# A two-layer convolution and attention kernel on one core: low halves in other groups, the projection bias in the norm, and a patch scratch ordered by row tile

## The chip, the core and the metric

The kernel runs on one core of a Trainium2 chip. TensorE (PE in the profile; PEld is its weight load), VectorE (DVE), ScalarE (ACT), GpSimd (POOL) and SyncE (SP) each work through their own list of instructions in order and meet at semaphores. DMAs are issued from SP and, for a few stores, from ACT; both kinds run on the same 16 DMA engines. The metric is the device time of one execution in microseconds, the median of several.

## The reference

Two layers on an image x of 384 channels by 192 by 192, in float32. Cut to what matters:

```python
# layer 0: x = x + L0(_gn(x)), _gn is a group norm over 32 groups of 12 channels
qkv = einsum('bchw,oc->bohw', x, w_qkv) + b_qkv          # 384 -> 1152 channels
qkv = qkv.reshape(b, 3*c, 96, 2, 96, 2).max(axis=(3, 5)) # 2 x 2 maximum
qkv = depthwise 3 x 3 convolution (w_dw) + b_dw
q, k, v = split(qkv, 3); q, k = q / norm(q), k / norm(k)
attn = einsum('bhcn,bhdn->bhcd', q, k) * temperature     # 8 heads of 48 channels
out = sum of 4 top-k softmaxes of attn, each @ v * a_i
out = gelu(out); out = repeat 2 x 2 of out; out = einsum('bchw,oc->bohw', out, w_proj) + b_proj
# layer 1: x = x + L1(_gn(x))
out = bn(dwconv 13 x 13) + bn(dwconv 3 x 3) + bn(x)      # depthwise, bn with given statistics
```

## The kernel before

The stages run one after another, with a barrier between them: the statistics of x, the affine part of the group norm (`group_affine`, "g0"), the q/k/v stage (`stage_qkv`), the attention matrix, the projection stage (`stage_project`), the second group norm ("g1"), the kernels and constants of the depthwise stage (`stage_kernels`), and the depthwise stage. All orders are written out by hand, as loops that every engine walks with its own waits.

**The q/k/v stage.** The image is cut into 24 tiles of 8 rows (1536 pixels). A step t handles two tiles, 2t and 2t+1, and there are 12 steps. A step has 36 slots, four for each of the 9 groups of 128 output channels. In slot s TensorE makes 18 matmuls (L724) of 384 columns into one of two banks `qbank[s % 2]`: two row pairs, three input blocks, and three products (high x high, high x low, low x high) since weights and pixels are split into two float16 halves, "high" and "low". It may start slot s when VectorE's maximum of slot s-2 is through. VectorE then does in slot s: the 2 x 2 maximum of the bank (`largest`, L631), one tap each of the two channel groups in work (`tap`, L644), and in six slots of the 36, given by `LOW_AT`, the low half of one input block (`low`, L623: xlo = xf - xhi). TensorE has more to do in some slots: the gram matmuls (`GRAM_AT`: behind slots 3 and 5) and the transposes of q and k behind slots 15, 19, 23, 27, 31 and 35.

One input block goes round a single buffer `xf[:, b]`: SP loads it (`load`, L298), ScalarE normalises it in place (`norm`, L472, slots by `NORM_AT`), writes its high half (`high`, L481, `HIGH_AT`), VectorE writes the low half, and this `lo_ready` lets SP load the same block of the next tile. ScalarE also does bias and tap 0 of every group (`first_tap`, L501 and L514), which VectorE's tap 1 waits for, the halo rows, the evacuation of the transposes (`turned`), and pieces of the 13 x 13 kernels (`bands`). In an entry `8: (0, 1)` of these tables 8 is the slot, 0 the half (tile 2t+2 or 2t+3) and 1 the block. Before the first step SP also fills most of the Toeplitz scratch in DRAM with zeros, six DMAs of 2048 runs each from `blank` (L426); in the before kernel they stand ahead of the loads of tile 2.

**The projection stage.** 24 steps of one tile of 8 rows. The list `ORDER` gives the sequence on TensorE and ScalarE. "A" n is attention times v into `abank[n]` and ScalarE's gelu of it (L1092, L1007); "Y" n is the projection into `ybank[n]` (L1101), three matmuls over the input blocks, and ScalarE's bias on it in place (L1010); "T" n is one of 12 runs of up to four 128 x 128 transposes (L1078) of the tile before (4, 4, 4 and 1 per channel block) into one of two banks `tbank[n % 2]`, and ScalarE's copy of it to `turned` (L995). T n on TensorE waits for the copy of T n-2. VectorE adds x and the projection for block b (four adds, L1027), when Y b has its bias and the four T of block b are through, then takes statistics (L1032). SP stores `turned` for each block to the patch scratch (L962), the copy of T 0, 4 or 8 waits until the store before of that block has landed, and SP loads v and x two tiles ahead (L891, L892) once the adds of the step are through.

**The depthwise stage.** 24 groups of 16 channels. A group is loaded from the patch scratch into `raw` in one DMA (`load_group`, L1199), two groups ahead; SP then issues one Toeplitz load per channel (L1293), eight channels ahead. TensorE makes 18 matmuls per channel (L1453) and nine fills of four transposes per group (L1434).

## Time and profile before

| | us |
|---|---|
| median of 3 runs | 3161.54 |
| lowest and highest run | 3158.27 and 3162.66 |
| the profiled execution, its own time | 3158.36 |
| its span, first to last instruction | 3156.6 |
| busy: PE, DVE, ACT | 2745.8, 2437.0, 1408.2 |
| mean DMA rate over the span | 179 GB/s |

A busy time is the union of an engine's instructions. Consecutive matmuls overlap in the records (one takes 0.33 us, and the next starts 0.16 us later), so PE's busy time counts the stream and not its single pieces. The stages are best read as stretches of the span: the q/k/v stage ends near 1640 us, the projection stage reaches from 1692 to 2130, and the depthwise stage begins at 2174.

### The profile page before, as it was taken

How to read it: one execution, taken by the hardware profiler on the slowest of the kernel's cores; microseconds unless marked ns; L12 is line 12 of the kernel's file. 1: busy time of each engine (PE TensorE's matmuls, PEld its weight loads, DVE VectorE, ACT ScalarE, POOL GpSimd, SP SyncE). 2: the span in 40 equal slices, each digit the busy share in tenths (PEclk: the TensorE clock that was granted, in tenths of full speed). 3: DMA queues.
4: the chain of work that ended last, by engine and by line, in shares of the span. 5: the costliest groups of instructions: out<-in, count | busy, mean ns of one | idle time of the engine just before them, and what ended most of it. 6: DMA issues, size and time to landing. Idle time of an engine off the chain costs nothing. (4 is left out here: it accounts for less than half of the span.)

```text
span 3156.6 us, 51308 instructions
## 1 busy us (share of the span) xinstructions
PE 2745.8 (87%) x18393; PEld 2009.8 (64%) x18393; DVE 2437.0 (77%) x3335; ACT 1408.2 (45%) x1799; POOL 27.5 (1%) x43
## 2 busy tenths in 40 slices
PE   0049999999999999999965888875999999999998
PEld 0035665665665665665643555544999999999998
DVE  7938899989989989999976888866666666666663
ACT  0024445455545555543223777773444444444442
POOL 0010000000000000000000000000000000000000
PEclk9999999999999999999987999986999999999999
DMA  9961112112112112111005999977999998889986
GB/s 359 415 239 60 47 41 81 55 50 82 54 50 82 54 50 82 54 49 36 16 19 193 324 319 318 327 253 212 279 283 277 281 284 283 280 276 282 283 254 185
DMA packets 231368, 565.73 MB, mean 179 GB/s; under 512 B 30928, under 2 KB 137008, under 8 KB 228144
## 3 DMA queue, kind: packets, MB, share of 16 engines
q1 hardware_dynamic: 213936, 496.89, 49.2%
q10 hardware_dynamic: 17280, 66.85, 5.6%
q8 instruction: 91, 1.49, 0.2%
q14 instruction: 61, 0.50, 0.1%
HBM read 402.95 MB, written 160.73 MB: 179 GB/s over the span
## 5 line engine op out<-in xcount | busy, mean ns | idle before, releaser
L1453 PE MATMUL cv_cb<-cv_hi,cv_toep 128*128 128x288 f16 (+1 forms) x4608 | 910.1, 290 | 31.6 <-DVE cv_lo L1387 29.0
L724 PE MATMUL qk_qb<-qk_xhi,whi 128*128 128x384 f16 x2592 | 847.9, 327 | 75.3 <-DVE qk_pool L631 61.0
L644 DVE SCALAR_TENSOR_TENSOR qk_dw<-qk_pool,qk_wd,qk_dw 128x768 f32<-128x768 f32 (+2 forms) x864 | 836.4, 1008 | 25.1 <-ACT qk_dw L514 25.0
L724 PE MATMUL qk_qb<-qk_xlo,whi 128*128 128x384 f16 x2592 | 847.3, 327 | 0.0
L724 PE MATMUL qk_qb<-qk_xhi,wlo 128*128 128x384 f16 x2592 | 847.0, 327 | 0.0
L1453 PE MATMUL cv_cb<-cv_lo,cv_toep 128*128 128x288 f16 (+1 forms) x2304 | 667.7, 290 | 0.0
L1453 PEld LDWEIGHTS cv_cb<-cv_hi,cv_toep 128*128 128x128 f16 x4608 | 523.1, 114 | 91.3 <-DVE cv_lo L1387 29.1
L631 DVE TENSOR_REDUCE qk_pool<-qk_qb 128x192 f32<-128x768 f32 x432 | 411.5, 953 | 111.0 <-PE qk_qb L724 99.7
L1341 ACT ACTIVATE cv_res<-cv_cb,cv_cst 128x288 f32<-128x288 f32 x384 | 191.8, 501 | 555.5 <-PE cv_cb L1453 555.5
L724 PEld LDWEIGHTS qk_qb<-qk_xhi,whi 128*128 128x128 f16 x2592 | 254.1, 98 | 252.9 <-DVE qk_pool L631 75.4
L1399 DVE COPY cv_rows<-cv_bb 128x512 f32<-128x512 f32 x216 | 145.9, 687 | 323.4 <-PE cv_bb L1434 323.4
L724 PEld LDWEIGHTS qk_qb<-qk_xhi,wlo 128*128 128x128 f16 x2592 | 254.3, 98 | 168.9 <-issue 2.0
L724 PEld LDWEIGHTS qk_qb<-qk_xlo,whi 128*128 128x128 f16 x2592 | 254.2, 98 | 160.5 <-issue 1.7
L1453 PEld LDWEIGHTS cv_cb<-cv_lo,cv_toep 128*128 128x128 f16 x2304 | 261.4, 113 | 28.0
L1387 DVE TENSOR_TENSOR cv_lo<-cv_raw,cv_hi 128x1300 f16<-128x1300 f32 x96 | 233.2, 2429 | 59.1 <-ACT cv_hi L1323 58.9
L1027 DVE TENSOR_TENSOR pr_x<-pr_xb,pr_yb 128x192 f32<-128x192 f32 (+1 forms) x288 | 213.9, 869 | 71.8 <-ACT pr_yb L1010 71.8
L995 ACT ACTIVATE pr_turned<-pr_tb 128x512 f32<-128x512 f32 (+1 forms) x300 | 243.9, 922 | 17.5 <-PE pr_tb L1078 17.5
L1323 ACT ACTIVATE cv_hi<-cv_raw 128x1300 f16<-128x1300 f32 x96 | 238.6, 2485 | 26.9 <-DVE cv_raw L1378 26.9
L501 ACT ACTIVATE qk_pool<-qk_pool,qk_bq 128x768 f32<-128x768 f32 x108 | 101.2, 937 | 322.4 <-DVE qk_pool L631 322.4
L521 ACT ACTIVATE qk_pool<-qk_pool 128x192 f32<-128x192 f32 x105 | 38.3, 365 | 391.5 <-DVE qk_dw L644 391.5
L1078 PE MATMUL pr_tb<-ident,pr_x 128*128 128x128 f32 x975 | 145.2, 282 | 47.7 <-ACT pr_turned L995 47.5
L1078 PEld LDWEIGHTS pr_tb<-ident,pr_x 128*128 128x128 f32 x975 | 116.7, 143 | 101.7 <-ACT pr_turned L995 62.9
(137 smaller groups left out, 2290.4 us busy)
## 6 DMA issues: line engine op xcount, KB each, us to landing
cv_toep<-toeplitz_scratch SPq DMA_DIRECT2D x384, 384.0 KB, 4.8
patch_scratch<-pr_turned SPq DMA_DIRECT2D x75, 832.0 KB, 7.9
cv_raw<-patch_scratch SPq DMA_DIRECT2D x24, 2600.0 KB, 10.9
st_x<-in_x SPq DMA_DIRECT2D x24, 2304.0 KB, 17.0
qk_xf<-in_x SPq DMA_DIRECT2D x72, 768.0 KB, 4.2
pr_xb<-in_x SPq DMA_DIRECT2D x24, 2304.0 KB, 9.8
out<-cv_rows ACTq DMA_DIRECT2D x72, 768.0 KB, 5.6
pr_vb<-v_scratch SPq DMA_DIRECT2D x24, 576.0 KB, 4.1
```

Source lines behind the costliest of these rows:

```text
L501: nc.scalar.activation(pool[:, o, 2:2 + UR, 1:1 + PW], pool[:, o, 2:2 + UR, 1:1 + PW], ACT.Identity, bias=bq[:, o:o + 1], scale=UNSCALE).t ...
L631: V.tensor_reduce(pool[:, o, 2 + j:4 + j, 1:1 + PW], qbank[s % NQB][:, :, 0:2 * W].rearrange("p j (r x c) -> p j x r c", r=2, c=2), AX.XY, ...
L644: V.scalar_tensor_tensor(acc, pool[:, o, r + y:r + y + n, x:x + PW], wd[:, o, k:k + 1], acc, ALU.mult, ALU.add).then_inc(taps_done, 1)
L724: ins = nc.tensor.matmul(qbank[s % NQB][:, h, 0:2 * W], w[:, b, o * P:(o + 1) * P], x[:, par, j // 2, b, at_row:at_row + 2 * W], start=n = ...
L995: nc.scalar.activation(turned[:, b, :, j:j + k].rearrange("p c j -> p j c"), tbank[n % 2][:, 0:k * P].rearrange("p (j c) -> p j c", j=k), ...
L1027: return nc.vector.tensor_tensor(out.rearrange("p (x c) y -> p y x c", c=2), x, low.unsqueeze(3).broadcast_to([P, n, PW, 2]), ALU.add)
L1078: ins = nc.tensor.transpose(tbank[n % 2][:, j * P:(j + 1) * P], x1[:, par, b, j0 + j].rearrange("p x y -> p (x y)"), ident[:, :])
L1323: nc.scalar.activation(hi[:, par, q * CPP:(q + 1) * CPP, :, 0:TI].rearrange("p c j i -> p (c j) i"), raw[:, par, :, q * CPP:(q + 1) * CPP, ...
L1341: nc.scalar.activation(res[:, par, :, :, c, :], cbank[c % NCB][:, 0:NPIX].rearrange("p (j b i) -> p b j i", b=NBAND, j=OJ), ACT.Identity, ...
L1387: V.tensor_tensor(half, raw[:, par, :, q * CPP:(q + 1) * CPP, :].rearrange("p i c j -> p (c j) i"), hi[:, par, q * CPP:(q + 1) * CPP, :, 0 ...
L1399: V.tensor_copy(dst, src).then_inc(rows_done, 1)
L1453: ins = nc.tensor.matmul(out, toep[:, c % NTOEP, :].rearrange("p (s m v) -> p s v m", s=NS, m=P)[:, s, u * 2 + part], x[:, par, c, u:u + O ...
```

## The change

There are four parts. In the q/k/v stage the six low halves go from slots 8, 10, 12, 24, 26 and 28 to slots 3, 5, 11, 19, 23 and 27, and norm, high and band pieces on ScalarE move with them: the norm of tile 2t+4 now falls in slots 33 to 35 of step t and its high half in slots 0 to 2 of the step after. Tile 2 is therefore loaded and normalised before the first step, and its loads stand ahead of the six blank DMAs; SP's stores of v are interleaved with the loads one by one. In the projection stage ScalarE's bias is gone: `x1` is kept without the projection bias, the bias `bp` is added to the channel means when the second group norm is computed (one more VectorE instruction), and the constant that layer 1 subtracts becomes mean - bp (a copy turned into a subtraction). `ORDER` spreads the transposes and the nine single matmuls of Y. The patch scratch is laid out [partition, row tile, group] in place of [partition, group, row tile]: a store of one block and partition is now one run of 6656 bytes, before 8 runs of 832; a load of one group and partition is now 25 runs of 832 bytes, before one of 20,800.

```diff
@@ group_affine
-            pe.wait_ge(chan_ready, CB)
+            pe.wait_ge(chan_ready, CB if offset is None else CB + 1)
...
+            if offset is not None:
+                V.tensor_tensor(chan[:, :, 0], chan[:, :, 0], offset[:, :], ALU.add).then_inc(chan_ready, 1)
+                dve.wait_ge(chan_ready, CB + 1)
@@ stage_qkv, sync
             for b in range(CB):
                 load(1, b)
+            for b in range(CB):
+                load(2, b)
             sp.wait_ge(blank_made, 1)
...
-            for b in range(CB):
-                load(2, b)
@@ stage_qkv, scalar
-            NORM_AT = {1: (0, 0), 2: (0, 1), 3: (0, 2), 17: (1, 0), 18: (1, 1), 19: (1, 2)}
-            HIGH_AT = {5: (0, 0), 6: (0, 1), 7: (0, 2), 21: (1, 0), 22: (1, 1), 23: (1, 2)}
+            NORM_AT = {13: (3, 0), 14: (3, 1), 15: (3, 2), 33: (4, 0), 34: (4, 1), 35: (4, 2)}
+            HIGH_AT = {0: (0, 0), 1: (0, 1), 2: (0, 2), 17: (1, 0), 18: (1, 1), 21: (1, 2)}
...
+            for b in range(CB):
+                norm(HALF, b)
             act.wait_ge(zeroed, 4)
@@ stage_qkv, vector
-            LOW_AT = {8: (0, 0), 10: (0, 1), 12: (0, 2), 24: (1, 0), 26: (1, 1), 28: (1, 2)}
+            LOW_AT = {3: (0, 0), 5: (0, 1), 11: (0, 2), 19: (1, 0), 23: (1, 1), 27: (1, 2)}
@@ stage_project, sync
-                            patch_dram[:, b * (P // GRP):(b + 1) * (P // GRP), bass.ds(t - 1, 1), :].rearrange("p g a n -> p g (a n)"),
-                            turned[:, b].rearrange("p (g c) j -> p g (c j)", c=GRP)).then_inc(stored[b], 16)
+                            patch_dram[:, bass.ds(t - 1, 1), b * (P // GRP):(b + 1) * (P // GRP), :].rearrange("p a g n -> p (a g n)"),
+                            turned[:, b].rearrange("p c j -> p (c j)")).then_inc(stored[b], 16)
@@ stage_project
-        ORDER = ("A0", "A1", "T0", "T1", "A2", "T2", "T3", "T4", "Y0", "T5", "T6", "Y1", "T7", "T8", "Y2", "T9", "T10", "T11")
+        ORDER = ("A0", "T0", "A1", "T1", "A2", "T2", "T3", "Y0", "T4", "Y1", "Y2", "T5", "Y3", "T6", "Y4", "T7",
+                 "Y5", "T8", "Y6", "T9", "Y7", "T10", "Y8", "T11")
@@ stage_project, scalar
-                    elif kind == "Y" and (inner or t < STEPS):
-                        act.wait_ge(proj_done, t * CB + n + 1)
-                        nc.scalar.activation(ybank[n][:, 0:PX], ybank[n][:, 0:PX], ACT.Identity,
-                                             bias=bp[:, n:n + 1]).then_inc(y_ready, 1)
@@ stage_project, vector
-                        dve.wait_ge(y_ready, t * CB + b + 1)
+                        dve.wait_ge(proj_done, t * CB + b + 1)
@@ stage_kernels
-            chained(V.tensor_copy(cst[:, :, 0], mean[:, :]))
+            chained(V.tensor_tensor(cst[:, :, 0], mean[:, :], bp[:, :], ALU.subtract))
@@ depthwise_start, load_group
-        sp.dma_start(raw[:, par].rearrange("p i c j -> p (i c j)"),
-                     patch_dram[:, bass.ds(g, 1), :, :].rearrange("p a i n -> p (a i n)")).then_inc(raw_in[par], 16)
+        sp.dma_start(raw[:, par].rearrange("p i c j -> p i (c j)"),
+                     patch_dram[:, :, bass.ds(g, 1), :].rearrange("p i a n -> p i (a n)")).then_inc(raw_in[par], 16)
```

VectorE in step 0 of the q/k/v stage, slots 7 to 10 before (line numbers of the before kernel; qk_xlo is a low half, qk_pool the maxima, qk_dw the taps):

```order
L631 TENSOR_REDUCE qk_pool<-qk_qb 128x2x96
L644 SCALAR_TENSOR_TENSOR qk_dw<-qk_pool,qk_wd,qk_dw 128x672
L631 TENSOR_REDUCE qk_pool<-qk_qb 128x2x96
L644 SCALAR_TENSOR_TENSOR qk_dw<-qk_pool,qk_wd,qk_dw 128x672
L623 TENSOR_TENSOR qk_xlo<-qk_xf,qk_xhi 128x1536
L631 TENSOR_REDUCE qk_pool<-qk_qb 128x2x96
L644 SCALAR_TENSOR_TENSOR qk_dw<-qk_pool,qk_wd,qk_dw 128x672
L631 TENSOR_REDUCE qk_pool<-qk_qb 128x2x96
L644 SCALAR_TENSOR_TENSOR qk_dw<-qk_pool,qk_wd,qk_dw 128x672 x2
L623 TENSOR_TENSOR qk_xlo<-qk_xf,qk_xhi 128x1536
```

The same engine and step after the change, from the low halves ahead of the stage through slots 0 to 7 (line numbers of the changed kernel, 8 higher here):

```order
L631 TENSOR_TENSOR qk_xlo<-qk_xf,qk_xhi 128x1536 x6
L639 TENSOR_REDUCE qk_pool<-qk_qb 128x2x96 x4
L631 TENSOR_TENSOR qk_xlo<-qk_xf,qk_xhi 128x1536
L639 TENSOR_REDUCE qk_pool<-qk_qb 128x2x96 x2
L631 TENSOR_TENSOR qk_xlo<-qk_xf,qk_xhi 128x1536
L639 TENSOR_REDUCE qk_pool<-qk_qb 128x2x96
L652 SCALAR_TENSOR_TENSOR qk_dw<-qk_pool,qk_wd,qk_dw 128x672
L639 TENSOR_REDUCE qk_pool<-qk_qb 128x2x96
L652 SCALAR_TENSOR_TENSOR qk_dw<-qk_pool,qk_wd,qk_dw 128x672
```

The low halves now stand behind the fourth and the sixth maximum, before they stood behind the ninth and the eleventh.

SyncE at the start of the q/k/v stage, before (qk_xf is an input block, L426 the blank DMAs):

```order
L298 DMA qk_xf<-in_x 128x1536 x3
L426 DMA toeplitz_scratch<-qk_blank 2048x1x448
L426 DMA toeplitz_scratch<-qk_blank 2048x1x704
L426 DMA toeplitz_scratch<-qk_blank 2048x1x448
L426 DMA toeplitz_scratch<-qk_blank 2048x1x704
L426 DMA toeplitz_scratch<-qk_blank 2048x1x448
L426 DMA toeplitz_scratch<-qk_blank 2048x1x704
L298 DMA qk_xf<-in_x 128x1536 x9
```

And after:

```order
L301 DMA qk_xf<-in_x 128x1536 x6
L431 DMA toeplitz_scratch<-qk_blank 2048x1x448
L431 DMA toeplitz_scratch<-qk_blank 2048x1x704
L431 DMA toeplitz_scratch<-qk_blank 2048x1x448
L431 DMA toeplitz_scratch<-qk_blank 2048x1x704
L431 DMA toeplitz_scratch<-qk_blank 2048x1x448
L431 DMA toeplitz_scratch<-qk_blank 2048x1x704
L301 DMA qk_xf<-in_x 128x1536 x6
```

Three input loads, those of tile 2, have gone from behind the six blank DMAs to ahead of them.

TensorE in step 1 of the projection stage, from T4 to T9, before (pr_tb are the transposes, pr_yb the projection, with bank numbers):

```order
L1078 MATMUL pr_tb0<-ident,pr_x1 128x128 x4
L1101 MATMUL pr_yb0<-pr_ge,pr_wp 128x384 x3
L1078 MATMUL pr_tb1<-ident,pr_x1 128x128 x4
L1078 MATMUL pr_tb0<-ident,pr_x1 128x128 x4
L1101 MATMUL pr_yb1<-pr_ge,pr_wp 128x384 x3
L1078 MATMUL pr_tb1<-ident,pr_x1 128x128
L1078 MATMUL pr_tb0<-ident,pr_x1 128x128 x4
L1101 MATMUL pr_yb2<-pr_ge,pr_wp 128x384 x3
```

And after, from Y0 to T7:

```order
L1104 MATMUL pr_yb0<-pr_ge,pr_wp 128x384
L1081 MATMUL pr_tb0<-ident,pr_x1 128x128 x4
L1104 MATMUL pr_yb0<-pr_ge,pr_wp 128x384 x2
L1081 MATMUL pr_tb1<-ident,pr_x1 128x128 x4
L1104 MATMUL pr_yb1<-pr_ge,pr_wp 128x384
L1081 MATMUL pr_tb0<-ident,pr_x1 128x128 x4
L1104 MATMUL pr_yb1<-pr_ge,pr_wp 128x384
L1081 MATMUL pr_tb1<-ident,pr_x1 128x128
```

The nine projection matmuls, three by three before, now stand between the transpose runs singly but for one pair.

## Rows read from the trace of the kernel before

**Rows 1.** Stretches: PE, PEld, DVE, ACT, POOL busy us (instructions), PEclk, DMA share, GB/s
```profile
188.00:1640.00 1452.00, 1376.42 (x8798) 861.49 (x8798) 1310.66 (x1369) 666.39 (x850) 0.00 (x0) 0.99 0.19 64
...
1692.00:2130.00 438.00, 380.56 (x1743) 251.40 (x1743) 345.68 (x509) 307.53 (x445) 0.27 (x3) 0.98 0.90 294
2130.00:2174.00 44.00, 8.07 (x37) 7.90 (x38) 19.74 (x42) 8.79 (x8) 4.69 (x10) 0.50 0.55 168
2174.00:3157.00 983.00, 971.94 (x7776) 880.59 (x7776) 587.20 (x1063) 406.06 (x478) 0.00 (x0) 0.99 0.88 270
```

**Rows 2.** Stretches that are steps 0, 1 and 3 of q/k/v, line L724 alone
```profile
188.50:329.31 140.81, 112.33 (x649) 64.84 (x650) 0.92 0.47 159
329.31:446.49 117.18, 107.30 (x649) 63.05 (x649) 1.00 0.16 51
...
563.73:682.09 118.36, 107.31 (x649) 62.96 (x648) 1.00 0.19 62
```

**Rows 3.** Waits in steps 1 to 10 of q/k/v: us, times, longest
```profile
PE qk_qb L724 <- DVE qk_pool L631: 35.5, 43, 1.1
```

**Rows 4.** Timelines of VectorE, slots 8 to 10, and TensorE, slot 15, of step 4
```profile
712.70 0.96 DVE L631 TENSOR_REDUCE qk_pool<-qk_qb 128x192 f32<-128x768 f32 x1
...
715.43 1.75 DVE L623 TENSOR_TENSOR qk_xlo<-qk_xf,qk_xhi 128x1536 f16<-128x1536 f32 x1
717.10 0.95 DVE L631 TENSOR_REDUCE qk_pool<-qk_qb 128x192 f32<-128x768 f32 x1
...
719.82 0.95 DVE L631 TENSOR_REDUCE qk_pool<-qk_qb 128x192 f32<-128x768 f32 x1
...
732.33 0.34 PE L724 MATMUL qk_qb<-qk_xhi,whi 128*128 128x384 f16 x1 [1.09 <-DVE qk_pool L631]
```

**Rows 5.** Timelines of SyncE, ScalarE and VectorE in step 0 of q/k/v
```profile
188.84 31.11 SPq L426 DMA_DIRECT2D toeplitz_scratch<-qk_blank  x6
...
234.59 3.46 ACT L472 ACTIVATE qk_xf<-qk_xf,qk_bx,qk_sx 128x1536 f32<-128x1536 f32 x2 [38.05 <-DMA qk_xf<-in_x]
...
241.75 0.92 DVE L644 SCALAR_TENSOR_TENSOR qk_dw<-qk_pool,qk_wd,qk_dw 128x672 f32<-128x672 f32 x1 [24.96 <-ACT qk_dw L514]
```

**Rows 6.** Waits of the projection stage, 1692 to 2130: us, times, longest
```profile
DVE pr_x L1027 <- ACT pr_yb L1010: 71.8, 24, 18.0
...
PE pr_tb L1078 <- ACT pr_turned L995: 47.5, 61, 1.0
```

**Rows 7.** Timeline of TensorE in one projection step
```profile
1894.90 3.49 PE L1092 MATMUL pr_ab<-pr_vb,pt 128*128 128x384 f32 x10 [0.24 <-issue]
...
1900.39 0.85 PE L1078 MATMUL pr_tb<-ident,pr_x 128*128 128x128 f32 x5
1902.18 0.66 PE L1078 MATMUL pr_tb<-ident,pr_x 128*128 128x128 f32 x4 [0.93 <-ACT pr_turned L995]
...
1911.69 0.33 PE L1078 MATMUL pr_tb<-ident,pr_x 128*128 128x128 f32 x1 [0.75 <-ACT pr_turned L995]
1911.86 3.42 PE L1092 MATMUL pr_ab<-pr_vb,pt 128*128 128x384 f32 x10
```

**Rows 8.** Timeline of VectorE in the same stretch, adds of two blocks
```profile
1892.96 2.96 DVE L1027 TENSOR_TENSOR pr_x<-pr_xb,pr_yb 128x192 f32<-128x192 f32 x4
...
1897.85 2.99 DVE L1027 TENSOR_TENSOR pr_x<-pr_xb,pr_yb 128x192 f32<-128x192 f32 x4
```

**Rows 9.** Stretches: x load, patch stores, group load, Toeplitz loads, one depthwise group
```profile
1888.00:1891.00 3.00, 3.00 (x16) 2.02 (x15) 2.96 (x4) 2.65 (x6) 0.00 (x0) 1.00 1.01 424
1896.00:1901.00 5.00, 5.00 (x25) 3.28 (x23) 4.80 (x8) 3.06 (x5) 0.00 (x0) 1.00 1.11 331
...
2503.00:2507.00 4.00, 4.00 (x35) 3.63 (x33) 0.69 (x1) 2.22 (x3) 0.00 (x0) 1.00 1.02 432
2509.00:2517.00 8.00, 8.00 (x67) 7.34 (x66) 7.86 (x19) 3.79 (x4) 0.00 (x0) 1.00 1.04 252
...
2500.40:2540.70 40.30, 40.30 (x326) 36.68 (x325) 24.73 (x45) 17.11 (x20) 0.00 (x0) 1.00 0.92 281
```

More of the change, by code:

```diff
@@ L84, in address, with group_affine @@
     return elements
-def group_affine(nc, tag, stats, member, mean, rstd, ahead=None):
+def group_affine(nc, tag, stats, member, mean, rstd, ahead=None, offset=None):
     with ExitStack() as ctx:
@@ L439, in step @@
                 prev = inner or t >= 1
+                more = inner or 2 * t + 3 < STEPS
                 if prev:
                     store(0)
-                    store(1)
-                if inner or 2 * t + 3 < STEPS:
+                if more:
                     load(t * 2 + 3, 0)
                 if prev:
+                    store(1)
+                if more:
+                    load(t * 2 + 3, 1)
+                if prev:
                     store(2)
-                if inner or 2 * t + 3 < STEPS:
-                    load(t * 2 + 3, 1)
+                if more:
                     load(t * 2 + 3, 2)
@@ L572, in step @@
                     if live and s in NORM_AT:
-                        h, b = NORM_AT[s]
-                        if inner or 2 * t + 2 + h < STEPS:
-                            norm(t * 2 + 2 + h, b)
+                        ahead, b = NORM_AT[s]
+                        if inner or 2 * t + ahead < STEPS:
+                            norm(t * 2 + ahead, b)
                     if live and s in HIGH_AT:
@@ L908, in project_start @@
     start = Shared()
[L909 removed]
+    start.vb, start.xb, start.x1, start.wp = vb, xb, x1, wp
     start.c_in, start.zeroed, start.v_in, start.x_in = c_in, zeroed, v_in, x_in
@@ L1095, in step @@
                     elif kind == "Y" and (inner or t < STEPS):
+                        o, b = n // CB, n % CB
                         if n == 0:
                             pe.wait_ge(gelu_done, t * CB + CB)
-                        if inner or t >= 1:
-                            pe.wait_ge(x1_done, t * CB - CB + n + 1)
-                        for b in range(CB):
-                            ins = nc.tensor.matmul(ybank[n][:, 0:PX], wp[:, b, n * P:(n + 1) * P], ge[:, b, :],
-                                                   start=b == 0, stop=b == CB - 1)
-                        ins.then_inc(proj_done, 1)
+                        if b == 0 and (inner or t >= 1):
+                            pe.wait_ge(x1_done, t * CB - CB + o + 1)
+                        ins = nc.tensor.matmul(ybank[o][:, 0:PX], wp[:, b, o * P:(o + 1) * P], ge[:, b, :],
+                                               start=b == 0, stop=b == CB - 1)
+                        if b == CB - 1:
+                            ins.then_inc(proj_done, 1)
             run(pe, step)
```

30 lines of the change are left out of this document (14 added, 16 removed).

## The prediction

> **What bounds the kernel now.** I read the stretches by stage first [rows 1], then inside each stage the waits and the timeline. The three long stages are three different cases. In the q/k/v stage TensorE is busy 1376 of 1452 us and VectorE 1311, with the DMAs at 0.19: two engines in lockstep. In the projection stage the DMA share is 0.90, TensorE has 381 of 438 us, VectorE 346, ScalarE 308: four resources near each other. In the depthwise stage TensorE is busy 972 of 983 us, so nothing else shortens it, but the DMAs are at 0.88, and that is what the new scratch order leans on.
>
> **Low halves, steps 1 to 10: -39 us.** TensorE's slot is 18 matmuls at 0.162 us, 2.92 us. VectorE's slot is 2.72 us (maximum to maximum, 717.10 to 719.82) and 4.40 with a low half (712.70 to 717.10) [rows 4]. TensorE starts slot s once the maximum of s-2 is through, so VectorE may lag by about 2.92 less the 0.95 of a maximum, 1.9 us. A low half adds 1.48 of lag, a plain slot gives back 0.2. Slots 8, 10, 12 build 1.5, 2.8 and then more, and TensorE stops, 1.09 us in the row shown [rows 4]; slots 24, 26, 28 repeat it. Steps 1 to 10 hold 43 such waits, 35.5 us [rows 3]. Three of them, about 1.1 us each, belong to the steps that are 1.2 us longer than their neighbours (118.36 against 117.18 [rows 2]), where the loop jumps; they stay. The other 40 leave 32.2 us, and each really costs 0.16 more, because a matmul's record ends 0.16 after the next could start: 38.6, say 39. After the change slots 3 and 5 also carry the gram matmuls, 12 each (some 2 us more on TensorE, so about 4.96 against 4.40: no lag at all), and 19, 23, 27 carry transposes (3.58 against 4.40: 0.8 of lag each, 0.2 per slot paid back, at most 1.3). Slot 11 has neither: lag 1.48, under 1.9. No wait is left. The hidden cost is on ScalarE: norm, high half and load now have to chain twice per step. The tightest place is block 2: low half done near 44 us into the step, its load lands some 4 us later, ScalarE wants it at 51 us behind the halo of slot 14. It holds with 3 us to spare. Bounds: -35 to -39.
>
> **Start of the stage: -25 us.** Step 0 takes 140.8 us [rows 2]. SP spends 31.11 us on the blank DMAs, tile 2 comes behind them, ScalarE's norm waits 38.05 us for it, bias and tap 0 queue behind that norm, and VectorE's first tap waits 24.96 us for tap 0 [rows 5]. After the change tile 2 goes first, and tap 0 of group 0 can be through at about 211 us, while VectorE wants it at 216. What is late next is tile 3, now the first load behind the blanks. They start some 9.6 us later (when the last low half of tile 1 is through), so block 0 of tile 3 lands at about 234.6 + 9.6 = 244 and block 2 at 248. ScalarE meets it in slot 13: three norms until 249.7, then tap 0 of group 3 until 251.6. VectorE wants that in slot 18, at about 253.4. It just fits. Bounds: 0 to -25, and I take the whole since the 1.8 us of room come from the same rows.
>
> **Projection: -29 us.** Here the steps are 16.96 us and 17.3 by turns (1894.90 to 1911.86 is a short one [rows 7]). TensorE's own work is about 14.8: two gaps, in front of T4 and T11, where it waits 0.93 and 0.75 us for ScalarE's copy [rows 7], cost 1.24 and 0.92 with the overlap of the records. They recur all through: 47.5 us in 61 waits, and VectorE waits 71.8 us on the bias in 24 waits [rows 6]. With T and Y interleaved a run comes about every 1.1 us, and a copy takes 1.05. More changes between transposes and matmuls cost some 0.05 us each, T4 still waits about 0.5. I count 15.2 + 0.5 + 0.2 for the loop's jump, 15.9. VectorE needs 4.9 per block (1892.96 to 1897.85 [rows 8]), 14.7. The DMAs: 2.95 MB of x and v at 424 GB/s is 7.0 us, 2.56 MB of stores at 331 is 7.7 [rows 9]; as long runs at 424 they take 6.0, so 13.0 in all plus a gap. A chain closes over two steps: the load goes out after the adds of block 2, the store of block 0 stands behind it and lands some 12 to 13 us after, ScalarE's copy T0 two steps on waits for it, then 5 to 6 us to VectorE's block 0 and 12.8 to the end of its block 2: about 31.5, 15.8 a step. So 15.9 against an average of 17.1, 22 steps, 26.6, and 2.5 from the last step: -29. Bounds: 14.7 (VectorE) gives -55, 17.1 gives 0.
>
> The Trainium skill, "DMA: Bandwidth & Descriptors", section "Specifications", says a transfer of at least 512 bytes already runs at line rate. By it 832-byte runs would lose nothing, the store term would be 0 in place of 1.7 us a step, and the loads of the next part would be free as well. The stretch of stores shows 331 GB/s beside 424 for the x load [rows 9], so the trace does not agree, and I go by the trace.
>
> **Group norm and constants: +0.2 us.** One VectorE instruction of three columns, in the chain to the first matmul of the norm. The dropped wait of ScalarE on the constants, the subtraction for the copy, and the 2 us longer load of group 0 (hidden by the 44 us of norm and kernels [rows 1]) cost nothing.
>
> **Depthwise: +1 us.** A group's load is 2.66 MB, now 432 GB/s, 6.2 us [rows 9]. The trace has no load of 832-byte runs. The nearest rows are the stores of that size, 331 GB/s, 8.0 us, and at the other end the Toeplitz loads, 252 GB/s, 10.6 us. One group of 40.3 us has a DMA share of 0.92 [rows 9], 3.2 us free. I take 8.0, by size the nearest: +1.8, which fits. The Toeplitz load issued right behind it has 16 us until its channel. Only at the start, where group 1 stands ahead of the third Toeplitz load, do I allow 1 us. Bounds: 0 to +26 (next paragraph).
>
> **Sum.** 3158.4 (the profiled execution's own time; its span is 1.8 less) - 39 - 25 - 29 + 0.2 + 1 = 3066.6. The median of before is 3.2 above that execution, so 3070.
>
> **Rivals.** (a) The depthwise stage becomes bound by its DMAs. At the Toeplitz rate the load is 10.6 us, 4.4 more, 1.2 over what is free, 22 groups: +26, 3096. For it: share 0.92, and the Toeplitz runs, three times as long as 832 bytes, get only 252. Against it: those read overlapping rows, and the share is above 1 in saturated stretches, so 0.92 overstates. Chance 0.12. (b) The stall of step 0 only moves: if tile 3 lands some 20 us later than I put it, or ScalarE's chain is longer, 3070 + 20 = 3090. Chance 0.06. (c) The projection keeps its period, since the two banks of T and ScalarE's copies set it and not the order: 3070 + 27 = 3097. The last steps, where T runs alone, speak for it. Chance 0.11. (d) The projection reaches VectorE's 14.7: 3044. Chance 0.07. (e) Slower than before: loads of 832-byte runs fall far below every row. It decides when a group's DMA time exceeds 40.3 by 4.2 us, 22 times 92: a load of 6.2 + 3.2 + 4.2 = 13.6 us, 196 GB/s. Nothing shows it. Chance 0.03, 3165 or more. (f) The tables move nothing that waits, because the waits in [rows 3] come from ScalarE's halo and not from the low halves: only -25 - 29, 3109. Rows 4 speak against it. Chance 0.02.
>
> The same page, section "How a descriptor splits into AXI transactions", cuts a run at 256-byte boundaries of its address; an 832-byte run that starts between them can cost up to 32 beats for 26. By that a load would be 6.2 x 32 / 26 = 7.6 us, an estimate. No row here shows it.
>
> **Chances and range.** My forecast 3070 has 0.59. A measurement of this kernel can tell about 0.2%, 6 us. Faster by more 0.96 (all but e, and the top end of a), within 0.01, slower 0.03. From 3044 to 3100 stand the forecast and a to d, some 0.9 with the edges cut.
>
> **What would show it.** Steps of q/k/v near 113.4 us and no wait of TensorE for the maxima; step 0 near 116 us with VectorE not waiting for tap 0, else (b). Projection steps of 15.9 us, no wait for a bias. In the depthwise stage TensorE at 40.3 us per group without a wait for cv_toep, else (a) or (e). I am wrong if a Toeplitz wait recurs each group or if ScalarE waits for qk_xf in each step.

## The result, and the profile after

The changed kernel takes 3066.43 us, the median of four runs (3061.8 to 3068.87), beside 3160.97 us for four runs of the kernel before (3158.27 to 3162.66) on the same chip. The ratio is 0.970 with a 95% interval of 0.9683 to 0.9717: faster, and 3.6 us below the forecast of 3070. The profiled execution took 3065.47 us, its span is 3063.8, against 3156.6 before: -92.8, where the prediction's own sum of stages has -91.8. One of the six executions of experiment 10 took 6945.88 us, more than double; nothing in the record explains it, and it is left out of that experiment's numbers.

The stretches by stage of the changed kernel; columns as in [rows 1]:

```profile
188.00:1576.00 1388.00, 1368.15 (x8798) 865.51 (x8798) 1313.96 (x1369) 665.30 (x850) 0.00 (x0) 0.99 0.20 67
1629.00:2033.00 404.00, 382.66 (x1743) 242.39 (x1743) 345.98 (x509) 281.79 (x373) 0.13 (x2) 0.97 0.85 319
2033.00:2076.00 43.00, 8.00 (x36) 7.83 (x36) 19.58 (x42) 8.66 (x8) 4.82 (x10) 0.50 0.63 157
2076.00:3063.00 987.00, 973.97 (x7776) 880.81 (x7776) 587.39 (x1064) 405.31 (x479) 0.00 (x0) 0.99 0.92 270
```

Beside [rows 1]: q/k/v 64 us shorter, projection 33 or so, norm and kernels about the same, depthwise 4.9 longer. TensorE's busy time has hardly moved in any stage. What went is its idle time. Measured from first matmul to first matmul:

| stretch | before | after | difference | forecast |
|---|---|---|---|---|
| first q/k/v matmul to first projection matmul | 1504.4 | 1440.6 | -63.8 | -64 |
| first projection matmul to the start of the norm | 436.9 | 403.8 | -33.1 | -29 |
| start of the norm to first depthwise matmul | 44.2 | 43.4 | -0.9 | +0.2 |
| first depthwise matmul to the end | 982.7 | 987.5 | +4.9 | +1 |

**q/k/v, the steps.** Steps 0, 1 and 2 of the changed kernel, the stretches of L732 alone, which answer to [rows 2]; and all waits of TensorE for the maxima from step 1 to the end of the stage, which answer to [rows 3]:

```profile
188.45:303.97 115.52, 109.89 (x649) 64.45 (x650) 0.99 0.57 194
303.97:417.43 113.46, 106.77 (x649) 63.48 (x649) 1.00 0.16 53
417.43:530.90 113.47, 106.78 (x650) 63.48 (x649) 1.00 0.19 64
```

```profile
PE qk_qb L732 <- DVE qk_pool L639: 2.1, 2, 1.2
```

A plain step goes from 117.18 to 113.46, and of 43 waits two are left, in steps where the loop jumps (a third such stop, 1.4 us, is filed by the profile under "issue"). VectorE works as much as before; only the places of its long pieces changed.

**q/k/v, the start.** SyncE, then ScalarE's norm of tile 3 and its tap 0 of group 3, and VectorE's taps of slot 18 in step 0 of the changed kernel, beside [rows 5]:

```profile
198.31 31.50 SPq L431 DMA_DIRECT2D toeplitz_scratch<-qk_blank  x6
```

```profile
244.54 1.67 ACT L478 ACTIVATE qk_xf<-qk_xf,qk_bx,qk_sx 128x1536 f32<-128x1536 f32 x1 [11.60 <-DMA qk_xf<-in_x]
...
250.81 0.95 ACT L520 ACTIVATE qk_dw<-qk_pool,qk_bd,qk_wd 128x672 f32<-128x672 f32 x1
```

```profile
252.04 1.74 DVE L652 SCALAR_TENSOR_TENSOR qk_dw<-qk_pool,qk_wd,qk_dw 128x672 f32<-128x672 f32 x2
```

The blank DMAs cost SyncE the same 31 us and start 9.5 us later. ScalarE still stops for an input, now tile 3, for 11.6 us in slot 13. But it has that time to spare: tap 0 of group 3 is through at 251.8, and VectorE, which in [rows 5] waited 24.96 us, does not wait for it. Of the two taps of slot 18 the second is the one that needs it, at 252.87. So a stall of 38 us became one of 11.6 that nobody sees.

**Projection.** Waits of the stage, beside [rows 6], and then SyncE and ScalarE in one step:

```profile
DVE pr_x L1030 <- PE pr_yb L1104: 38.5, 24, 16.9
...
ACT pr_turned L1003 <- DMA patch_scratch<-pr_turned: 36.0, 20, 3.7
...
PE pr_tb L1081 <- ACT pr_turned L1003: 14.2, 30, 1.2
```

```profile
1838.20 0.43 SPq L899 DMA_DIRECT2D pr_xb<-in_x  x1
1838.85 8.40 SPq L969 DMA_DIRECT2D patch_scratch<-pr_turned  x3
```

```profile
1850.19 1.09 ACT L1003 ACTIVATE pr_turned<-pr_tb 128x512 f32<-128x512 f32 x1 [1.92 <-DMA patch_scratch<-pr_turned]
```

TensorE's waits for ScalarE's copy fell from 47.5 us in 61 to 14.2 in 30. VectorE's wait for the projection, 71.8 us on the bias before, is 38.5. A new wait stands in their place: ScalarE's copy T0 waits for the store of the same block that went out behind the loads, here 11.3 us earlier. The steps from 1 on take 15.7 us on average, (358.35 - 12.95) / 22, where before they took 17.1.

**Depthwise, the start.** SyncE and TensorE in group 0, then stretches around TensorE's stop (PE, PEld, DVE, ACT, POOL, PEclk, DMA share, GB/s):

```profile
2088.60 0.59 SPq L1203 DMA_DIRECT2D cv_raw<-patch_scratch  x1
2089.23 33.94 SPq L1297 DMA_DIRECT2D cv_toep<-toeplitz_scratch  x16
```

```profile
2101.77 0.40 PE L1457 MATMUL cv_cb<-cv_hi,cv_toep 128*128 128x288 f16 x1 [5.22 <-DVE cv_lo L1391]
```

```profile
2096.27:2101.77 5.50, 0.29 (x3) 0.03 (x1) 5.43 (x13) 1.61 (x3) 0.00 (x0) 0.85 1.09 286
2101.77:2105.77 4.00, 4.00 (x17) 2.43 (x18) 1.39 (x6) 0.00 (x0) 0.00 (x0) 0.50 1.04 250
2105.77:2109.77 4.00, 4.00 (x29) 3.23 (x27) 0.59 (x1) 3.24 (x3) 0.00 (x0) 0.85 1.05 251
```

The kernel before has the same stop at the same matmul, shorter:

```profile
2197.35 0.29 PE L1453 MATMUL cv_cb<-cv_hi,cv_toep 128*128 128x288 f16 x1 [2.59 <-issue]
```

Before the change the granted clock was 1.00 (2.4 GHz) in the 4 us behind that stop. Behind the 5.5 us of the changed kernel it was 0.50, that is 1.2 GHz, for 4 us, and then 0.85: 17 matmuls where 4 us at full clock hold some 32. The longer stop costs 2.6 us and the slow clock some 2.3, which is the 4.9 of the table. It is no accident of one execution: where this one waits 5.22 us, the kernel of experiment 8, with the same order of loads, waits 5.84, and has 0.52 in the 4 us behind; that of experiment 6, with the old scratch, waits 3.02 us and has 1.00. The profile names VectorE's low half as the releaser, but the last low half of group 0 was through at 2088.6, before the stop began; that is also when SyncE could issue the load of group 2, and the Toeplitz load of channel 8, which TensorE needed at 2096.3, went out behind it. A group in the steady part takes 40.3 us as before. The load of a group, now in runs of 832 bytes, can be seen there by itself:

```profile
2490.00:2497.00 7.00, 7.00 (x58) 6.39 (x57) 1.98 (x4) 3.74 (x4) 0.00 (x0) 1.00 1.11 358
```

At 358 GB/s its 2.66 MB take 7.4 us.

### The profile page after: what moved, and what is told of

Same layout as the page of the kernel before. It is cut to its first block and busy times, and to the rows that moved or that the text cites. A ratio compares the mean times of both kernels' runs of the same rounds, so it can differ in the third digit from the quotient of the medians.

```text
span 3063.8 us, 51236 instructions
## 1 busy us (share of the span) xinstructions
PE 2741.7 (89%) x18393; PEld 2004.9 (65%) x18393; DVE 2440.7 (80%) x3336; ACT 1380.7 (45%) x1727; POOL 27.4 (1%) x43
## 5 line engine op out<-in xcount | busy, mean ns | idle before, releaser
L732 PE MATMUL qk_qb<-qk_xhi,whi 128*128 128x384 f16 x2592 | 846.5, 327 | 20.5 <-DVE qk_xlo L631 14.3
L732 PE MATMUL qk_qb<-qk_xlo,whi 128*128 128x384 f16 x2592 | 846.5, 327 | 0.0
L732 PE MATMUL qk_qb<-qk_xhi,wlo 128*128 128x384 f16 x2592 | 846.3, 326 | 0.0
L732 PEld LDWEIGHTS qk_qb<-qk_xhi,whi 128*128 128x128 f16 x2592 | 254.0, 98 | 183.9 <-DVE qk_xlo L631 17.4
L732 PEld LDWEIGHTS qk_qb<-qk_xhi,wlo 128*128 128x128 f16 x2592 | 254.0, 98 | 168.4 <-issue 1.4
L732 PEld LDWEIGHTS qk_qb<-qk_xlo,whi 128*128 128x128 f16 x2592 | 254.0, 98 | 162.9 <-issue 1.0
L1003 ACT ACTIVATE pr_turned<-pr_tb 128x512 f32<-128x512 f32 (+1 forms) x300 | 257.6, 918 | 87.1 <-PE pr_tb L1081 50.7
L1030 DVE TENSOR_TENSOR pr_x<-pr_xb,pr_yb 128x192 f32<-128x192 f32 (+1 forms) x288 | 214.4, 871 | 38.5 <-PE pr_yb L1104 38.5
L1081 PE MATMUL pr_tb<-ident,pr_x 128*128 128x128 f32 x975 | 161.8, 283 | 15.5 <-ACT pr_turned L1003 14.2
```

What stands on the lines that cost most here:

```text
L732: ins = nc.tensor.matmul(qbank[s % NQB][:, h, 0:2 * W], w[:, b, o * P:(o + 1) * P], x[:, par, j // 2, b, at_row:at_row + 2 * W], start=n = ...
L1003: nc.scalar.activation(turned[:, b, :, j:j + k].rearrange("p c j -> p j c"), tbank[n % 2][:, 0:k * P].rearrange("p (j c) -> p j c", j=k), ...
L1030: return nc.vector.tensor_tensor(out.rearrange("p (x c) y -> p y x c", c=2), x, low.unsqueeze(3).broadcast_to([P, n, PW, 2]), ALU.add)
L1081: ins = nc.tensor.transpose(tbank[n % 2][:, j * P:(j + 1) * P], x1[:, par, b, j0 + j].rearrange("p x y -> p (x y)"), ident[:, :])
```

## The experiments

Each kernel was timed against the kernel before on the same chip. A stretch or a period comes from its one profiled execution, a time in us from the median of its runs. "A0" is the first attention matmul of a projection step. The experiments ran on four chips, where the kernel before has medians of 3160.56 to 3163.99 us, so the difference of two kernels timed on different chips is uncertain by some 3 us, and the stretches of the traces are the surer measure. They vary too: the five kernels whose projection stage is that of the changed kernel take 357.5 to 361.4 us from first to last A0.

**1. The q/k/v part alone (qkv_alone).** The kernel before with `stage_qkv` of the changed kernel, no other edit; of its diff:

```diff
+            for b in range(CB):
+                load(2, b)
             sp.wait_ge(blank_made, 1)
...
-            LOW_AT = {8: (0, 0), 10: (0, 1), 12: (0, 2), 24: (1, 0), 26: (1, 1), 28: (1, 2)}
+            LOW_AT = {3: (0, 0), 5: (0, 1), 11: (0, 2), 19: (1, 0), 23: (1, 1), 27: (1, 2)}
```

> The kernel before with the changed q/k/v stage alone (tables, tile 2 ahead of the blank DMAs, interleaved stores of v). My theory: the parts are independent, so this gives exactly the q/k/v term, -64 us: 3097 us, steps of 113.5 us from step 1 on and 115.5 for step 0, projection still at 16.95 and 17.3 us by turns, depthwise unchanged. Rival: part of the gain seen in the full change comes from the lighter stages behind it (SyncE and ScalarE work that overlaps the end of the stage): then 3105 us or more.

Measured: 3096.13 us, ratio 0.979 (0.9773 to 0.9806). First q/k/v matmul to first A0: 1439.1, against 1440.6 in the full change. Projection 389.5 from first to last A0, 390.2 before; depthwise 982.8, 982.7 before. The parts add, and some 70% of the gain is here.

**2. Low halves in slots 8, 10 and 11 (lows_8_10_11).**

```diff
-            LOW_AT = {3: (0, 0), 5: (0, 1), 11: (0, 2), 19: (1, 0), 23: (1, 1), 27: (1, 2)}
+            LOW_AT = {8: (0, 0), 10: (0, 1), 11: (0, 2), 19: (1, 0), 23: (1, 1), 27: (1, 2)}
```

> The changed kernel with the first three low halves in slots 8, 10 and 11 in place of 3, 5 and 11; nothing else moves. My lag model (a low half adds 1.48 us of lag to VectorE, a plain slot gives back 0.2, TensorE stops above 1.9): slot 10 ends at 2.76, so a stall of 0.9 us, slot 11 adds 1.5; 2.3 to 2.7 us a step in 11 steps: +26 to +29, 3092 to 3095 us, with two waits of TensorE for the maxima in each step. Rival: the waits came from ScalarE's halo and other work, not from the place of the low halves: within 5 us of 3066.

Measured: 3094.04 us, ratio 0.9778 (0.9762 to 0.9795). Waits of TensorE from step 1 on, and step 1 by L732 alone:

```profile
PE qk_qb L732 <- DVE qk_pool L639: 23.8, 22, 1.3
```

```profile
303.77:419.61 115.84, 107.12 (x650) 63.32 (x649) 1.00 0.17 52
```

Two low halves, put into slots where TensorE has nothing extra, cost 2.4 us a step (115.84 against 113.46), where the lag model gave 2.3 to 2.7; 22 waits in 11 steps are its two a step. The time from first q/k/v matmul to first A0 is 24.9 us longer: step 0 came out 1 us shorter than in the changed kernel. The rival, waits that come from ScalarE's halo (f of the prediction), is out.

**3. Tile 2 behind the blank DMAs again (tile2_behind).**

```diff
-            for b in range(CB):
-                load(2, b)
             sp.wait_ge(blank_made, 1)
...
+            for b in range(CB):
+                load(2, b)
```

> The changed kernel with the three loads of tile 2 put back behind the six blank DMAs (the norm of tile 2 still ahead of the first step). My theory of the start: ScalarE waits again for the input until about 234 us, tap 0 comes at about 242, step 0 goes back from 115.5 to about 140 us: +25, 3091 us. Rival: the gain of step 0 came from the tables and not from the place of the loads: within 5 us of 3066.

Measured: 3103.01 us, ratio 0.9805 (0.9788 to 0.9821); the stage is 35.1 us longer, not 25. VectorE and TensorE in step 0:

```profile
241.62 1.76 DVE L631 TENSOR_TENSOR qk_xlo<-qk_xf,qk_xhi 128x1536 f16<-128x1536 f32 x1 [34.86 <-ACT qk_xhi L487]
```

```profile
244.31 0.50 PE L732 MATMUL qk_qb<-qk_xhi,whi 128*128 128x384 f16 x1 [32.69 <-DVE qk_pool L639]
```

The direction is as expected and the place is not. With the new tables the first low half of the loop stands in slot 3, so tile 2 is wanted in slot 3 and no longer in slot 8. VectorE now stops there, 34.9 us, ahead of where it used to stop for tap 0. So the preload and the tables are one edit: with the new tables, a late tile 2 costs 35 us, where the stall it caused in the kernel before was 25.

**4. The old sequence, without the bias (old_order).** The changed kernel with, where Y is now a single matmul, the sequence of the kernel before:

```diff
-        ORDER = ("A0", "T0", "A1", "T1", "A2", "T2", "T3", "Y0", "T4", "Y1", "Y2", "T5", "Y3", "T6", "Y4", "T7",
-                 "Y5", "T8", "Y6", "T9", "Y7", "T10", "Y8", "T11")
+        ORDER = ("A0", "A1", "T0", "T1", "A2", "T2", "T3", "T4", "Y0", "Y1", "Y2", "T5", "T6", "Y3", "Y4", "Y5",
+                 "T7", "T8", "Y6", "Y7", "Y8", "T9", "T10", "T11")
```

> The changed kernel with the sequence of the kernel before in the projection stage (three projection matmuls together, A0 A1 T0 T1 A2 ...), the bias still folded away. My theory, TensorE's gaps come from the sequence: the gap in front of T4 (1.24 us) stays since no bias stands before it, the one in front of T11 (0.92) goes with the bias in part; period 16.2 to 16.6 us, 3080 to 3090 us. Rival: ScalarE's bias was the cause of everything, and the sequence is worth nothing: 3066 us. Second rival: the sequence is worth all: 3100 us.

Measured: 3099.16 us, ratio 0.98 (0.9784 to 0.9817), first to last A0 389.4 us, steps of 16.91 and 17.25 by turns.

```profile
PE pr_tb L1081 <- ACT pr_turned L1003: 43.3, 54, 1.1
...
DVE pr_x L1030 <- PE pr_yb L1104: 70.0, 24, 17.6
```

My expectation of 3080 to 3090 missed, and the second rival was right. Under the old sequence the bias on ScalarE and the new scratch, which this kernel has too, were together worth 0.8 us in 23 steps. VectorE, which waited 71.8 us for the bias, now waits 70.0 for TensorE. Both gaps in front of T4 and T11 stayed (0.92 and 0.72 us in a step), so neither came from the bias.

**5. The new sequence, with the bias (bias_kept_before).** The kernel before, with the new `ORDER` and the single matmuls of Y; ScalarE's bias follows the last of each three:

```diff
-                    elif kind == "Y" and (inner or t < STEPS):
-                        act.wait_ge(proj_done, t * CB + n + 1)
+                    elif kind == "Y" and n % CB == CB - 1 and (inner or t < STEPS):
+                        o = n // CB
+                        act.wait_ge(proj_done, t * CB + o + 1)
```

> The kernel before with the new sequence of the projection stage alone (ScalarE's bias kept, old scratch, old q/k/v stage). My theory: with transposes and single matmuls interleaved ScalarE's copies have the time they need, also with the bias between them; period 15.8 to 16.4 instead of 17.1, 23 steps, -16 to -30: 3131 to 3145 us. Rival: the bias holds ScalarE and VectorE back whatever the sequence, 3155 us or more.

Measured: 3142.99 us, ratio 0.9934 (0.9918 to 0.9951), first to last A0 375.5 us, 14.7 less than before, steps between 15.3 and 18.6. The time lies inside the 3131 to 3145 that I gave; the mean step, 16.45, is just above the 15.8 to 16.4.

```profile
ACT pr_turned L996 <- DMA patch_scratch<-pr_turned: 42.9, 17, 3.3
```

The sequence alone brings less than half of the projection's 31.9 us, and it brings it up to the wait for the stores. The rival that the two banks and the copies keep the period whatever the sequence (c of the prediction) is out.

**6. The old scratch (old_scratch).** The changed kernel with the stores, the group load and the two address steps as before:

```diff
-    patch_dram = nc.dram_tensor("patch_scratch", [P, TI, NG, GRP * TJ], F32).ap()
+    patch_dram = nc.dram_tensor("patch_scratch", [P, NG, TI, GRP * TJ], F32).ap()
```

> The changed kernel with the old order of the patch scratch [partition, group, row tile] (stores of 832-byte runs, group loads of 20,800-byte runs). My theory, the two-step cycle of load, store and copy in the projection stage: stores at 331 instead of 424 GB/s lengthen that cycle by 0.6 to 1.7 us per two steps, the period goes from 15.6 to 15.9 to 16.4 us, +7 to +20 us; and the start of the depthwise stage gives 4.9 us back: 3068 to 3081 us. Rival: the length of the runs does not matter to the cycle, the period stays at 15.6 and only the depthwise start changes: 3061.5 us.

Measured: 3068.78 us, ratio 0.9701 (0.9685 to 0.9717). First to last A0 363.4 us against 358.35 (15.9 a step where I gave 15.9 to 16.4), and the depthwise stage 982.9, so 4.6 us of its loss come back. The two cancel: the medians of this kernel and of the changed one can't be told apart, the stages of the two traces can.

With 4 to 6 the projection's gain divides so, first to last A0: sequence -14.7, then the bias -12.1, then the scratch -5.1, in that order of doing them. Each figure is of one trace, and with the spread of 357.5 to 361.4 the scratch's share can be 2 to 6. In another order the shares differ, since bias and scratch without the sequence give 0.8.

**7. The store ahead of the loads (store_first).** SyncE issues the store of block 0, then the loads of v and x, then the other two stores.

```diff
                             turned[:, b].rearrange("p c j -> p (c j)")).then_inc(stored[b], 16)
-                if inner or t + 2 < STEPS:
...
-                    sp.wait_ge(att_done, t * CB + CB)
-                    sp.wait_ge(x1_done, t * CB + CB)
-                    start.load(sp, t + 2, par)
+                        if b == 0 and (inner or t + 1 < STEPS):
...
+                            sp.wait_ge(att_done, t * CB)
+                            sp.wait_ge(x1_done, t * CB)
+                            start.load(sp, t + 1, 1 - par)
```

> The changed kernel, in which SyncE issues the store of channel block 0 ahead of the loads of v and x and not behind them, in every projection step. My theory: the period of 15.6 us is the two-step cycle in which the copy T0 waits for that store (36.0 us in 20 waits); with the store ahead of 2.95 MB of loads the wait goes, and the period falls to about 15.0, between TensorE's and VectorE's 14.7: -13 us, 3053 us. Rival: the wait moves to the later blocks or to the loads (the DMAs have a share of about 0.9): 3063 to 3070 us.

Measured: 3057.79 us, ratio 0.9667 (0.9651 to 0.9683), 8.6 us under the changed kernel; first to last A0 350.0, 8.3 less. Every step from 1 on takes 15.2 to 15.35 us. The wait of ScalarE for a store, and TensorE in one step from the end of A2 to T5:

```profile
ACT pr_turned L1003 <- DMA patch_scratch<-pr_turned: 0.9, 1, 0.9
```

```profile
1817.04 0.71 PE L1081 MATMUL pr_tb<-ident,pr_x 128*128 128x128 f32 x5
1817.79 0.91 PE L1104 MATMUL pr_yb<-pr_ge,pr_wp 128*128 128x384 f32 x2
1818.80 0.66 PE L1081 MATMUL pr_tb<-ident,pr_x 128*128 128x128 f32 x4
1819.29 1.46 PE L1104 MATMUL pr_yb<-pr_ge,pr_wp 128*128 128x384 f32 x4
```

The wait went from 36.0 us in 20 to one of 0.9: the two-step cycle of load, store and copy did set the period. The period stopped at 15.3, though, not at 15.0. Y0 takes 0.65 us of the stream, yet T4 starts 1.01 after it, at 1818.80, with ScalarE's copy of T2: 0.36 us lost in each step.

**8. And Y1 ahead of T4 (order_y1).** Store as in 7, and one swap in `ORDER`:

```diff
-        ORDER = ("A0", "T0", "A1", "T1", "A2", "T2", "T3", "Y0", "T4", "Y1", "Y2", "T5", "Y3", "T6", "Y4", "T7",
+        ORDER = ("A0", "T0", "A1", "T1", "A2", "T2", "T3", "Y0", "Y1", "T4", "Y2", "T5", "Y3", "T6", "Y4", "T7",
```

> The changed kernel with the store of block 0 ahead of the loads (as in store_first) and with Y1 moved in front of T4 in the sequence. My theory: in store_first the period of 15.31 us is TensorE's stream plus a stop of 0.36 us in front of T4, which waits for ScalarE's copy of T2; with one more projection matmul (0.65 us) ahead of T4 the stop goes, period 14.95, 23 steps, -8 us against store_first: 3050 us. Rival: the period then is set by VectorE or by ScalarE's chain of gelu and copies, and stays above 15.2: 3056 us or more.

Measured: 3050.12 us, ratio 0.965 (0.9637 to 0.9662), steps of 14.95 and 15.0.

```profile
1813.31 1.56 PE L1104 MATMUL pr_yb<-pr_ge,pr_wp 128*128 128x384 f32 x4
1814.71 0.60 PE L1081 MATMUL pr_tb<-ident,pr_x 128*128 128x128 f32 x4
1815.14 0.81 PE L1104 MATMUL pr_yb<-pr_ge,pr_wp 128*128 128x384 f32 x2
```

Now 1.40 us lie between the starts of Y0 and T4, two projection matmuls of 0.65 and 0.1 us more. One swapped pair is worth 7.3 us from first to last A0.

**9. The load of group 2 later (group2_later).** In group 0 alone, ahead of channel 12's Toeplitz load and not channel 8's.

```diff
-                    if c == GRP // 2 and (inner or g + 2 < NG):
+                    if c == (3 * GRP // 4 if at(g, 0) else GRP // 2) and (inner or g + 2 < NG):
```

> The changed kernel, in which SyncE issues the load of group 2 ahead of the Toeplitz load of channel 12 and not of channel 8, in group 0 alone. My theory: TensorE's stop of 5.5 us at channel 8 of group 0, and the 2.4 us at the lower clock behind it, come from the Toeplitz load of channel 8 that stands behind the 2.66 MB of group 2 in SyncE's queue: both go, -7.9 us, 3058.5 us. Rival: the stop belongs to the load of group 1, whose 3200 runs hold the DMA engines up, or to the low halves of group 0: 3066 us.

Measured: 3061.02 us, ratio 0.9671 (0.9655 to 0.9687); depthwise 981.4 instead of 987.5, -6.1.

```profile
2109.12 0.29 PE L1457 MATMUL cv_cb<-cv_hi,cv_toep 128*128 128x288 f16 x1 [1.58 <-issue]
```

The stop at channel 8 is gone, and with it the slow clock (1.00 in the 4 us where channel 8 begins). A smaller one came at channel 12, now the first behind the group load: the missing 1.8 us. That it follows the place of the load settles what TensorE waited for, whatever releaser the profile names.

**10. Groups 1 and 2 placed anew (groups_early).** Group 1 is loaded right behind group 0, ahead of the norm; group 2 ahead of channel 14's Toeplitz load.

```diff
         load_group(sp, 0, 0)
+        load_group(sp, 1, 1)
...
-                    if at(g, 0) and c == 2:
-                        start.load_group(sp, 1, 1)
-                    if c == GRP // 2 and (inner or g + 2 < NG):
+                    if c == (GRP - 2 if at(g, 0) else GRP // 2) and (inner or g + 2 < NG):
```

> The changed kernel; the load of group 1 goes out right behind that of group 0, ahead of the norm, and that of group 2 ahead of the Toeplitz load of channel 14 of group 0. My theory: no Toeplitz load of the first group stands behind a group load that it cannot afford; both stops of TensorE go (5.5 us in the changed kernel, 1.9 us left in group2_later), the depthwise stage takes 979.5 us instead of 987.5: -8, 3058 us. Rival: the 2.66 MB of group 1 slow the small DMAs of norm and kernels, the first matmul comes some us later and eats the gain: 3062 us or more.

Measured: 3056.32 us, ratio 0.9667 (0.9655 to 0.968); depthwise 980.0, no stop left in group 0, and the first depthwise matmul no later (43 us behind the norm's start).

**11. Edits 8 and 10 together (combined).**

The edits are the diffs of 7, 8 and 10.

> All three edits together (store of block 0 first, Y1 ahead of T4, groups 1 and 2 placed as in groups_early). The stages are separated by barriers, so the gains add: 3066.4 - 8.6 (store_first) - 8 - 8 = 3042 us. Rival: the stores that end the projection stage are now closer to the group loads, and 3 us or more are lost: 3045 us or more.

Measured: 3041.0 us (3038.1 to 3043.64), ratio 0.9619 (0.9606 to 0.9631): the fastest of all, 25 us under the changed kernel. The gains add, as barriers between stages let one expect. In the depthwise stage one wait of TensorE above 0.6 us is left, the one for its first matmul:

```profile
PE cv_cb L1456 <- DVE cv_lo L1390: 28.0, 1, 28.0
```

**12. The same, with the old scratch (combined_old).**

Kernel 11 with the edit of 6.

> The kernel 'combined' with the old order of the patch scratch (stores of 832-byte runs, group loads of 20,800-byte runs). My theory: a projection step has 14.95 us, and the DMAs then need 7.0 us for the loads and 7.7 for the stores, 14.7: still inside, but with no slack, so the period is between 14.95 and 15.4, 0 to +10 us; the depthwise stage is bound by TensorE either way, 0. I expect 3041 to 3050 us, most likely 3046. Rival: with the wait for the store out of the chain the layout is worth nothing at all, within 2 us of 3041. Second rival: the group loads of long runs help the start of the depthwise stage, 3038 us or less.

Measured: 3068.27 us, ratio 0.9708 (0.9695 to 0.9721): 27 us slower, where I had allowed 10. First to last A0 is 366.3 us against 344.6, and that is nearly all of the 22.2 us between the two profiled executions. The same 260 us of the steady projection stage in kernel 11, in this one and in that of experiment 6, and a like stretch of the kernel before:

```profile
1700.00:1960.00 260.00, 258.42 (x1223) 167.81 (x1222) 248.13 (x363) 198.75 (x259) 0.00 (x0) 1.00 1.00 365
```

```profile
1700.00:1960.00 260.00, 245.43 (x1137) 155.21 (x1136) 230.29 (x337) 181.06 (x241) 0.00 (x0) 1.00 1.03 339
```

```profile
1700.00:1960.00 260.00, 252.51 (x1163) 158.42 (x1164) 234.71 (x343) 184.99 (x246) 0.00 (x0) 1.00 1.04 345
```

```profile
1760.00:2030.00 270.00, 242.19 (x1127) 160.70 (x1126) 226.45 (x332) 194.86 (x285) 0.00 (x0) 1.00 0.98 321
```

With stores of 832-byte runs the DMA engines are busy all the time at 339 to 345 GB/s: a step moves 5.5 MB, and two sequences as different as those of 6 and 12 gave 15.9 and 16.1 us. With 6656-byte runs kernel 11 moves 365 GB/s in steps of 15.0. Its TensorE is busy 258.4 of 260 us and its DMA share is 1.00, so neither has anything to speak of to spare. The kernel before already stood at 0.98.

How the traffic of one step divides shows in the traces, where the loads and the stores run nearly one after the other. First the loads of v and x of a step of the kernel before, whole, and their last 2 us; then, from the changed kernel, a stretch of stores alone:

```profile
1885.00:1893.00 8.00, 8.00 (x40) 5.47 (x40) 5.80 (x10) 5.53 (x8) 0.00 (x0) 1.00 0.99 346
1891.00:1893.00 2.00, 2.00 (x11) 1.29 (x10) 1.86 (x5) 1.27 (x3) 0.00 (x0) 1.00 1.04 304
```

```profile
1848.00:1853.00 5.00, 4.66 (x22) 2.82 (x20) 4.77 (x7) 3.08 (x6) 0.00 (x0) 1.00 1.02 426
```

The stores go at 426 GB/s in long runs and at 331 in short ones [rows 9]: 6.0 and 7.7 us a step, as the prediction had it. The loads take 8 us and more, not 7.0: 424 GB/s [rows 9] is the rate in the middle of the x load, and its last 2 us run at 304.

## Why the prediction held, and where not

**Low halves: right, step and size.** -39 was forecast as 113.4 us a step, and 113.46 came; what follows step 0 is 38.5 us shorter. The model behind it (1.48 of lag for a low half, 0.2 given back by a plain slot, a bound of 1.9) put experiment 2 at 2.3 to 2.7 us a step and two waits; 2.4 and two came. The total was 24.9 us, just under the 26 to 29 I gave.

**Start: right.** Forecast -25, measured 140.81 to 115.52, -25.3. Tile 3's block 0 was put at 244 and ScalarE took it at 244.54; tap 0 of group 3 at 251.6, and it ended at 251.8. So the chain came as forecast and rival (b) did not. The room was smaller, though: VectorE wanted that tap at 252.87 and not at 253.4, so it was 1.1 us and not 1.8. With the same q/k/v code other kernels took 113.7 to 115.6 us for step 0. What I had not seen is that the tables also bring forward the time at which tile 2 is wanted; the prediction had no term for it, the expectation of experiment 3 did, and missed by 10 us.

**Projection: the direction and one mechanism right, two terms wrong.** The period was put at 15.9 and measured 15.7 on average; 26.6 us forecast for the steps, 31.9 measured from A0 to A0; 2.5 for the last step, 1.2 measured. The two-step cycle was put at about 31.5 us. It is there: the copy T0 at 1834.36 starts behind one store and the one two steps on, at 1865.59, behind another, 31.2 us, and experiment 7 takes it away. But I used it as a check and built the 15.9 on TensorE's stream, 15.2 + 0.5 + 0.2. Once the cycle is gone that stream gives 15.3, so my 15.9 for TensorE was too long by 0.6, and the cycle was the real bound at 15.6. Each part was too large: experiment 8 shows the stream without the stop at 14.95 to 15.0 where I had 15.2 (the changes between transposes and matmuls, for which I had 0.4, cost 0.2 at most), the stop in front of T4 was 0.36 and not 0.5, and the loop's jump does not show in its steps.

The other wrong term is the loads' 7.0 us. It did not enter the sum of 15.9, but it made the DMAs look as if 14.7 us were enough for a step of the old scratch, and experiment 12 was forecast with it. The 7.0 came from the fastest stretch of the x load. Whole, the packets of v and x take 8.3 to 8.8 us of the 16 engines' time a step in the traces. The lower end, with 7.7 for the stores, makes 16.0, which is what experiments 6 and 12 have (15.9 and 16.1); with 6.0 for long stores it is 14.3 to 14.8, near the 15.0 of kernel 11. So the new scratch is worth only 0.2 us a step in the changed kernel (15.9 against 15.7), where the cycle holds the period, and 1.1 once the cycle and the stop are gone (16.1 against 15.0). Rival (d), VectorE's 14.7, did not come even there. The Trainium skill's rule ("DMA: Bandwidth & Descriptors", "Specifications"), line rate from 512 bytes on, would have made the new scratch worth nothing; the runs disagree, with stores at 331 GB/s in 832-byte runs and at 426 in 6656-byte runs. The prediction had set stores beside loads; this sets stores beside stores.

**The bias: wrong as a reason.** The 71.8 us that VectorE waits for the bias in [rows 6] looked like a cost. VectorE had that time to spare, for in experiment 4 the bias is gone, VectorE waits 70.0 us for TensorE instead, and nothing is gained. Only when the sequence lets TensorE run ahead is ScalarE's time worth something.

**Norm and kernels: nothing lost, as forecast, and a little gained.** +0.2 forecast, -0.9 measured. From the norm's start to the first depthwise matmul the three kernels with the old norm take 43.9 to 44.4 us and the eleven with the new one 43.2 to 43.8, so a gain of about half a microsecond or more is real. Which edit brings it was not tried.

**Depthwise: the stage right, the start mis-sized.** No wait recurs in the groups, 40.3 us each, so rivals (a) and (e) are out; the DMA share of a group rose from 0.92 to 0.95. The load of a group takes 7.4 us at 358 GB/s where I took 8.0 from the stores' 331: loads and stores of the same 832-byte runs do not go at the same rate. The term "only at the start ... do I allow 1 us" should have been 4.9, and it named the wrong place: group 1 ahead of the third Toeplitz load. The stop is at channel 8, behind group 2. The prediction's "has 16 us until its channel" does not hold in group 0: there the load of group 2 went out at 2088.6 and TensorE reached channel 8 at 2096.3, 7.7 us later. I had not looked for a stop in the trace of before: its 2.6 us at that very matmul were the sign that there was no room for a slower group load. The slower granted clock behind the stop then nearly doubled the price.

The misses nearly cancel in the sum: some 4 us too little gain in the projection, 4 too little loss in the depthwise stage. That is luck. The 64 us of q/k/v are not.

## What to carry to other kernels

Two engines in lockstep over two banks have a lag that can be computed: write down what each slot adds and gives back, and put long pieces only where the other engine has extra work. A large wait in a list is worth nothing until the engine that waits is the bound, so undo one part at a time before you name a cause. Where a DMA share is above 0.9, find out how long a step's whole traffic takes, first byte to last and not at its fastest rate, before you speed up the engines, and look at the first group of a pipeline by itself: a small load queued behind a large one stops the bound engine there and nowhere else.
